# One PSUM group for the first gates, with the table load and the third w2 sum moved in the opening of sequence 0

## The reference

```python
def absmean_quant(w):
    scale = jnp.mean(jnp.abs(w))
    mask = (jnp.abs(w) >= scale * 0.7).astype(w.dtype)
    return jnp.sign(w) * mask

i_pre = soft_cap(x @ Wig.T + big)      # soft_cap(x) = 15 * tanh(x / 15)
f_pre = soft_cap(x @ Wfg.T + bfg)
# per step of the scan: f_log = log_sigmoid(f_t); m_new = max(f_log + m, i_t) ...
x = x + L0_attn_ref(layernorm(x), ...)                       # heads, norm, sigmoid gate, Wout
h = gelu(einsum('bsd,fd->bsf', layernorm(x), w1_q) + b1)     # w1_q, w2_q = absmean_quant(w1), (w2)
x = x + einsum('bsf,df->bsd', h, w2_q) + b2
```

## Time and profile before

| | us |
|---|---|
| median of 3 runs | 1740.26 (1739.93 to 1741.75) |
| time of the profiled execution | 1742.3 |
| span in the profile | 1740.6 |
| PE busy | 1707.5 |
| DVE busy | 1437.6 |
| ACT busy | 1059.6 |

### The profile page before, as it was taken

The page is one execution under the profiler, slowest core; times in us unless marked ns, Lnnn a source line. Parts: engine busy times, 40 slices in busy tenths (PEclk is TensorE's granted clock), DMA queues, the critical chain, the costliest instruction groups (busy, mean ns, idle before and its releaser), DMA issues.

```text
span 1740.6 us, 31380 instructions
## 1 busy us (share of the span) xinstructions
PE 1707.5 (98%) x12028; PEld 841.4 (48%) x12028; DVE 1437.6 (83%) x2528; ACT 1059.6 (61%) x1769; POOL 606.6 (35%) x477
## 2 busy tenths in 40 slices
PE   6899999999999999999999999999999999999999
PEld 4554445444444444445444444444444444454455
DVE  7888788897888978789887888988789788886872
ACT  6978375473746638375573746648375573847643
POOL 1242514335241442514235241442514235241430
PEclk9999999999999999999999999999999999999999
DMA  8736253442725326253442725336262442625120
GB/s 321 219 89 167 58 141 72 117 120 56 170 60 127 87 80 160 58 154 59 120 117 56 171 60 126 87 92 152 55 161 61 110 119 56 148 59 132 33 55 25
DMA packets 294981, 187.45 MB, mean 108 GB/s; under 512 B 239136, under 2 KB 260640, under 8 KB 289712
## 3 DMA queue, kind: packets, MB, share of 16 engines
q1 hardware_dynamic: 293248, 182.30, 41.7%
q10 hardware_dynamic: 1584, 3.15, 0.5%
HBM read 96.47 MB, written 20.23 MB: 67 GB/s over the span
## 4 chain that ended last, share of the span: by engine, by line
PE 81%; DVE 8%; DMA 3%; SPq 3%; issue 2%; POOL 1%; ACT 1%; POOLq 0%; DVEq 0%; ACTq 0%
PE pf L2073 24%; PE pf L2057 22%; PE pa L1926 17%; PE pa L1902 7%; PE psh L1926 5%; SPq L530 2%; PE psh L2013 2%; DMA kT<-shared 1%; PE psh L1968 1%; PE psh L2047 1%; DVE gT L1633 1%; PE pa L2013 1%; DVE dec L1482 1%; PE pa L1893 1%; PE psh L2009 1%
## 5 line engine op out<-in xcount | busy, mean ns | idle before, releaser
L2073 PE MATMUL pf<-w2T,gT 128*128 128x512 f16 x2048 | 505.8, 379 | 0.0
L2057 PE MATMUL pf<-x2T,w1T 128*128 128x512 f16 x1920 | 422.0, 379 | 0.0
L2057 PEld LDWEIGHTS pf<-x2T,w1T 128*128 128x128 f16 x1920 | 185.4, 98 | 222.5
L2073 PEld LDWEIGHTS pf<-w2T,gT 128*128 128x128 f16 x2048 | 195.5, 97 | 177.0
L1633 DVE SCALAR_TENSOR_TENSOR gT<-g,wscale,gT 128x512 f16<-128x512 f32 x240 | 208.5, 871 | 22.5 <-ACT gT L1046 20.2
L1926 PE MATMUL pa<-wT,xT 128*128 128x512 f16 x960 | 212.8, 379 | 0.6 <-ACT sig L970 0.6
L1043 ACT ACTIVATE g<-pf,b1c 128x512 f32<-128x512 f32 x240 | 164.1, 684 | 72.5 <-PE pf L2057 56.6
L1046 ACT ACTIVATE gT<-g,wscale 128x512 f16<-128x512 f32 x240 | 173.3, 722 | 7.9
L1926 PE MATMUL pa<-wT,shared 128*128 128x512 f16 x768 | 176.2, 379 | 1.6 <-DMA shared<-qT 0.8
L1051 ACT ACTIVATE ktok<-kT 128x512 f32<-128x512 f32 x64 | 40.4, 631 | 216.4 <-DVE kT L1528 214.9
L1902 PE MATMUL pa<-xT,wT 128*128 128x512 f16 x768 | 171.4, 379 | 0.0
(11 more groups left out here) (246 smaller groups left out, 2705.2 us busy)
## 6 DMA issues: line engine op xcount, KB each, us to landing
dec<-gate_r SPq DMA_DIRECT2D x32, 1024.0 KB, 6.1
xin<-L_attn_x SPq DMA_DIRECT2D x16, 1024.0 KB, 6.0
out<-x1b SPq DMA_DIRECT2D x64, 256.0 KB, 2.3
xres<-L_attn_x SPq DMA_DIRECT2D x16, 512.0 KB, 4.3
xres<-L_attn_x SPq DMA_DIRECT2D x32, 256.0 KB, 3.0
qw<-gate_w SPq DMA_DIRECT2D x128, 48.0 KB, 2.0
s<-state_w SPq DMA_DIRECT2D x60, 97.5 KB, 2.4
qw<-kT SPq DMA_DIRECT2D x120, 48.0 KB, 2.0
```

Source lines behind the costliest of these rows:

```text
L2057: last = nc.tensor.matmul(bank, w1T[:, k, tok(f)], x2T[:, part, :, k, :], start=(k == 0 and part == HI), stop=(k == KD - 1 and part == LO))
L2073: last = nc.tensor.matmul(bank, gT[:, part, f, tok(t)], w2T[:, f, :], start=(f == 0 and part == HI), stop=(f == NF - 1 and part == LO), sk ...
```

## The change

- ACT runs a small `Square` of a constant first, so that the activation table is loaded before the first weights have landed. `sum_squares(G_QK)` moves from the third place to behind the weights of V and the gate.
- PE's `maxima` is split in two (`peak_transpose`, `peak_sums`), with other work between the halves, and DVE's `bounds` gives its first half to `row_maxima`.
- For sequence 0, `first_gates` sums all 12 products in one group of 32 rows of PSUM. ACT's `first_exponents` reads that by tanh straight from PSUM, makes |tanh| and exp(-15|tanh|). `gate_copy`, the three additions of `gate_sum` and the two instructions of `gate_minus` are gone for sequence 0.
- `absolute_sums2(0, 1)` follows `first_exponents`; the third sum of w2, `absolute_sums2(2)`, goes behind the late decays and `weights_hi(USES_O[2])`; `absolute_sums1(6)` goes behind the weights of QK; `queries(0, 1)` comes before `absolute_sums1(7, 0)`.
- On DVE the low halves of the gate weights come after two of V's four, `gate_one` and `gate_rest` are pulled out of `gate_logs`, and the four of QK follow `scales(LATER, 2)` in one piece.

Core of the diff:

```diff
+            def first_exponents():
+                bank = pa_bank(0, U_GATE)
+                act.wait_ge(pa_fill, pa_filled(0, U_GATE))
+                nc.scalar.activation(th, pa[0:GROWS, bank, :], ACT.Tanh, bias=gate_bias[:, 0:1],
+                                     scale=evac[0:GROWS, W_GATE:W_GATE + 1]).then_inc(tanh_ok, 1)
+                act.wait_ge(tanh_ok, 1)
+                nc.scalar.activation(ge, th[0:NH, :], ACT.Abs).then_inc(pa_free[bank], 1)
+                act.wait_ge(pa_free[bank], pa_done(0, U_GATE))
+                nc.scalar.activation(ge, ge, ACT.Exp, scale=-CAP).then_inc(gate_act, 1)
...
             def opening():
-                gate_copy(0)
-                absolute_sums2(1, 2)
-                gate_tanh(0)
+                first_exponents()
+                absolute_sums2(0, 1)
                 value(0, 0)
-                gate_exp(0)
-                absolute_sums1(6, early=True)
+                gate_log(0)
                 weights_hi(*USES_QK[0:3])
...
+            act.wait_ge(s_pchain, 1)
+            nc.scalar.activation(hinv[:, :], half[:, :], ACT.Square).then_inc(s_table, 1)
             sum_squares(G_V)
             sum_squares(None)
-            sum_squares(G_QK)
...
             replace_rows(G_V)
-            absolute_sums2(0)
+            sum_squares(G_QK)
...
+            def first_gates():
+                bank = take_pa(0, U_GATE)
+                for k in range(KD):
+                    for n, (ws, xs) in enumerate(PARTS):
+                        last = nc.tensor.matmul(bank[0:QUAD, :], wgT[:, k, ws, :], xT[:, xs, :, k, :],
+                                                start=(k == 0 and n == 0), stop=(k == KD - 1 and n == 2))
+                last.then_inc(pa_fill, 1)
```

More of the change, by code:

```diff
@@ L1179, in largest, with row_maxima @@
                                         apply_absolute_value=True).then_inc(s_peak, 1)
-            def bounds(cols, step):
+            def row_maxima(step):
                 dve.wait_ge(s_rows, step)
@@ L1188, in bounds @@
                                         ALU.mult).then_inc(s_rowmax, 1)
+            def bounds(cols, step):
+                known = PEAK_COLS[step - 1]
+                n = known.stop - known.start
                 dve.wait_ge(s_allmax, step)
@@ L1770, in _ @@
             split_lo(2, 3)
-            weights_lo(*USES_V)
+            weights_lo(*USES_V[0:2])
             weights_lo(USE_GATE)
+            weights_lo(*USES_V[2:4])
             largest()
-            gate_sum(0)
+            first_floor()
+            row_maxima(2)
+            gate_one(0)
             bounds(LATER, 2)
+            gate_rest(0)
+            scales(LATER, 2)
+            weights_lo(*USES_QK)
             sequence(0, None, True)
@@ L1812, in weights, with peak_transpose @@
                     last.then_inc(s_wfill, 1)
-            def maxima(sums, peak_count, step):
+            def peak_transpose(sums, peak_count, step):
                 pe.wait_ge(s_sums, sums)
@@ L1821, in maxima, with peak_sums @@
                 nc.tensor.transpose(peak_rows[0:n, :], peak[:, known], ident[:, :]).then_inc(s_rows, 1)
+            def peak_sums(step):
+                n = PEAK_COLS[step - 1].stop - PEAK_COLS[step - 1].start
                 pe.wait_ge(s_rowmax, step)
@@ L2172, in opening @@
                 weights_ready(USE_GATE)
-                gates(0)
-                weights(*USES_QK[0:2])
+                first_gates()
                 weights_ready(*USES_V)
                 tokens(0, U_V, xT[:, :, 0, :, :], C_V)
-                maxima(3, 1, 2)
-                weights(USES_QK[2])
+                peak_transpose(3, 1, 2)
+                weights(USES_QK[0])
+                peak_sums(2)
+                weights(*USES_QK[1:3])
                 late_values(0, 1)
@@ L2246, in _ @@
             weights(*USES_V)
+            peak_transpose(2, 0, 1)
             transposes(0, 1)
-            maxima(2, 0, 1)
+            peak_sums(1)
             transposes(2, 3)
```

51 lines of the change are left out of this document (26 added, 25 removed).

## The result

| | before | after |
|---|---|---|
| median, us | 1740.10 (1739.43 to 1741.75, 20 runs) | 1743.06 (1741.72 to 1745.22, 20 runs) |
| time of the profiled execution | 1742.3 | 1743.28 |
| span in the profile | 1740.6 | 1741.5 |

The account below looks back on a forecast made before the run. PE is busy 98% of the span; in the opening, late decays and ACT's sums meet at DVE near 60.5 us. Tanh 0, landing 0, third sum +1.90, cover 0 gave +1.9: 1744.2 us (1742.2 against the median), range 1739.2 to 1744.9.

Parts of the forecast that it names:

- Part 1: Gates and tanh in the opening: tanh at about 25 instead of 29.36, i rows' DMA issued at 25.7 instead of 30.09.
- Part 2: Earlier issue of the i rows: buys 0 (-1.05 to +0.3), landing kept at 39.4 behind the 1 MB load.
- third case: Rival: i rows not held by the load ahead, DVE's 1.05 us idling goes; +0.85, or 1741.1 us; chance 0.12.
- Part 3: Third w2 sum moved into ACT's full stretch behind the late decays: +1.90 us, last sum ending at 62.4.
- Part 4: Remaining edits, acting before 46 us, hidden by idling of PE (1.14 us) and ACT (2.07): 0 (0 to +0.4).
- The clock rival: PE idles 2.5 us ahead of the third output gate group, its clock falls: +4.4, or 1744.7 us; chance 0.14.
- The sum: All terms together: +1.9 us (0.2 to 3.3), 1744.2 against the profiled execution, 1742.2 against the median.

Follow-up runs that it names:

- e9: Kernel before, with the DMA of the i rows issued ahead of the load of the next sequence: 1740.47 us, ratio 0.9998.
- e2: Kernel before, with only the third w2 sum moved from ahead of the tanh to behind the late decays and third O weight: 1742.68 us, ratio 1.0011.
- e11: Changed kernel with eight unused matmuls on PE in each of two gaps, ahead of the fourth O weight's transposes and the third output gate group: 1742.77 us, ratio 1.0013.
- e3: Changed kernel with the third w2 sum put back beside the first and second, ahead of the values: 1743.73 us, ratio 1.0017.
- e1: Changed kernel run again with no edit: 1744.75 us, ratio 1.0023.
- e4: Changed kernel with the first w2 sum ahead of the tanh, second and third behind the exponents, none behind the late decays: 1743.72 us, ratio 1.0022.
- e6: Changed kernel with the DMA of the i rows issued ahead of the load of the next sequence: 1741.95 us, ratio 1.0009.
- e8: Changed kernel with the edits of both e4 and e6: 1741.92 us, ratio 1.0008.
- e5: Changed kernel with eight unused matmuls on PE ahead of the transposes of the fourth O weight: 1742.34 us, ratio 1.0013.
- e7: e4 plus DVE making the low half of the first O weight before its wait for the i rows: 1743.91 us, ratio 1.0021.
- e10: e8 with ACT reading the first two output gates earlier, after three and five sums of w1: 1741.24 us, ratio 1.0006.

## Why the prediction held, point by point

**Part 1** held. The gates started at 20.98 (20.6 estimated) and took 4.78 us (4.1): by the prediction's 0.21 us for each at the lower level, nine or ten of the twelve ran there and not seven. The tanh came at 25.80 (25) and the DMA of the i rows at 26.59 (25.7).

**Part 2** was right in its result, and its reason was half right. The landing hardly moved: DVE started at 38.81 against 39.45. The prediction said that the i rows stand behind the load of 1 MB, and the order at SP does count: behind the load they landed between 38.7 and 40.3, ahead of it between 36.2 and 37.1 (the table at e9). But "behind" is not the strict order that it read from the landings. In the changed kernel the load was issued at 20.41 and took 19.7 us, so it landed at 40.1, 1.3 us after DVE had started on the i rows:

```profile
xin<-L_attn_x SPq DMA_DIRECT2D x1, 1024.0 KB, 19.7
```

So the order of landings in the earlier trace rows, 39.2 and 39.45, was no rule. This trace agrees with the rule that the prediction cited from the Trainium skill, "DMA: Bandwidth & Descriptors", Queues, rings and completion order, that completion isn't first in, first out. Within either order the landing does not follow the issue: behind the load the i rows were issued between 24.5 and 30.1 us, ahead of it between 25.0 and 30.0. That is why an earlier tanh bought next to nothing. How the transfers share the engines, and what holds the i rows for the 6 to 11 us that are left with no load ahead of them, stays open.

The third case, "the i rows land early", came in part: 0.64 of its 1.05 us.

**Part 3** held, and is the best supported: +1.90 forecast, a reduction 1.98 later in e2, and medians of +1.86 in e2 and +2.2 in e11 (each with an interval of 0.3 or 0.7 to over 3 us). The places in the profile after are those forecast: `xres` at 46.42 (47) without idling, the keys at 48.31, the reduction at 61.97 (62.5) after 2.31 us of idling (1.9), the third output gate group at 59.34 (59.8). The 0.5 by which they are early is Part 2's 0.64. One sentence was wrong in what it left out: "only change places" hid that the fourth sum had covered the first queries, as e3 showed.

**Part 4** is the term that was mis-sized. It gave the cover 0 to 0.4 us and counted PE's idling of 1.14 at 46 as cover for PE being late. It did not ask what PE being early does. In before PE had idled from 44.92 until 46.06; in e1 it idled from 43.65 until 45.69, so PE was 1.27 earlier there and what it waited for only 0.37, and the clock fell. The first profile of the same kernel has no such gap, and its gates ended 1.66 later than e1's (25.76 against 24.10); in e4, with the largest gap (3.25), they ended at 23.65. So how late the gates end goes along with the gap, though which part of the new order makes PE early was not tried apart. Filling the gap was worth 2.3 us against e1 and about 1.3 against the result's 20 runs (+1.6 against +2.96), with intervals that overlap.

**The clock rival** stood at the wrong place for the changed kernel as profiled: 0.50 was expected at 58 to 62 in its case, and both profiles of the kernel have the fall absent there. e4, e6 and e8 show that the place is real, with 4.41 to 4.45 us for a group of 2.76. Its price was put too high: 1.7 us and not 2.5, since the clock came back within the group.

**The sum.** Third sum +1.9 to +2.2 (e2, e11); what remains to +2.96 is 0.8 to 1.1, and it is not seen when the gap at 46 is filled (e5) or both are (e11), though it is no larger than these intervals are wide. A cause for it is shown in one profile, e1, and e3 lost as much with no fall at all; how many executions have the fall can't be read from their times. The five variants without the third sum behind the late decays and with no matmuls added (e3, e4, e7, e8, e10) are still at +0.6 to +3.2, so the third sum and the gap at 46 are not the whole account of the new order. The median says +2.96, inside the range. Against the profiled execution the forecast was 1744.2 and 1743.28 came, too high by 0.9; against the median it was 1742.2 and 1743.06 came, too low by 0.9. That the two misses are of the same size is chance, and so is part of the good fit: the sum holds nothing for the 0.8 to 1.1 us, and the range was wide enough to take it in. In the pair of profiles 0.7 of what is missing is the 0.88 us instruction of before, which the later reduction no longer meets.

## What to carry to other kernels

An instruction moved into a stretch of an in-order engine that has no hole puts off all behind it by its full distance of starts, and a step taken from ahead of a transfer that lands at the same time in any case gives nothing. When such a step comes earlier and what it feeds does not, ask which engine now runs ahead and where it will stand: on PE that idle time has a price of its own, the clock of what comes after. Before a work item is called free to swap with its neighbour, name what it covers at its old place, since the reverse edit in another order is not the reverse in time. And when a step behind a transfer doesn't move, look whether its engine idled ahead of it: without idle time its start says nothing about the landing (e9).

## What the runs showed of the hardware that was not expected

- A DMA of 16 KB issued behind one of 1 MB from the same queue had landed 1.3 us before it (the profile after). Issued ahead of it, it landed at 36.2 to 37.1 in five profiles, and behind it at 38.7 to 40.3 in nine, whenever it was issued between 24.5 and 30.1.
- After idle times of much the same length PE's clock fell or didn't. It was at the lower level after 2.04, 2.08 and 3.25 us (e1, e6, e4), and at full clock after 1.92 us (the profile after), 2.06 and 2.45 us (e10). Ahead of the third output gate group PE idled 2.13 us in four profiles: the clock fell in e4 and e8 (4.41 and 4.45 us for the group) and stayed in e1 and e3 (2.76). So the length of the idle time alone does not say which it will be; why is open.
- An instruction of DVE on 128x2 elements took 0.88 us in before, 0.65 in e9 and 0.91 in e7, and 0.17 in the other eleven profiles. In those three, and in no other, POOL was at work on `qw` beside it, and in each it ended with POOL's instruction: 62.49 and 62.47 in before, 61.98 and 61.94 in e9, 63.36 and 63.34 in e7. The reciprocal just ahead of it, beside the same POOL instruction, took 0.17. That fits a wait until POOL is done; no run moved POOL's instruction by itself. The Trainium skill, "Trainium Architecture — The Big Picture", What this means for kernel authors, says that VectorE and GpSimd contend for a shared port pair, as an exclusive lock; the three profiles agree with it. The rows of POOL in before, e7 and after, and of DVE in e7:

```profile
60.65 1.81 POOL L670 TENSOR_TENSOR qw<-qw,qT 128x768 f32<-128x768 f32 x1 [4.86 <-DVE qw L1431]
```

```profile
61.53 1.81 POOL L671 TENSOR_TENSOR qw<-qw,qT 128x768 f32<-128x768 f32 x1 [5.73 <-DVE qw L1450]
```

```profile
62.45 0.91 DVE L1274 TENSOR_SCALAR w<-w 128x2 f32<-128x2 f32 x1
```

```profile
59.73 1.81 POOL L671 TENSOR_TENSOR qw<-qw,qT 128x768 f32<-128x768 f32 x1 [3.10 <-DVE qw L1450]
```
